# Clears of the retention heads' row tiles set between POOL's copies, and the heads' sums of squares and absolute totals made on POOL

## The chip, the cores and the metric

The kernel runs on one core of a Trainium2 chip. The metric is the time of one execution in microseconds (us), less is better. The core's engines work side by side and are tied by semaphores: PE (matmul; its weight loads are listed as PEld), DVE (vector), ACT (activation), POOL (GpSimd) and SP, which here issues DMAs. All tensors are float32.

## The reference, cut to what matters

The program is a chain of small layers over 2048 tokens of 128 channels: a causal attention layer, a spline layer, the retention layer (`L0_attn_b`), the spline layer again, linear attention, and two blocks of causal attention with a mixture of experts round an RWKV layer. The change is inside the retention layer, which computes

```python
q, k = split(x @ W_qk + b_qk);  v = x @ W_v + b_v          # 16 heads: 8 wide for q and k, 16 wide for v
mask = decay / sqrt(decay.sum(-1))                          # causal, one decay rate for each head
scores = einsum('bhtd,bhsd->bhts', q, k) * mask
denom = clip(abs(scores).sum(-1), 1.0, 50000.0)             # one absolute total for each token and head
ret = einsum('bhts,bhsv->bthv', scores / denom, v)
ret = ret * rsqrt(mean(ret * ret, axis=-1) + EPS)           # mean over the 16 values of a head
out = ((x @ W_g + b_g) * ret) @ W_o + b_o
```

The kernel puts the decays into q and k. It takes `ret` without the denominator, by a running state, and brings `denom` in at the end.

## The kernel before

`retention_layer` works on `NT` = 16 tiles of 128 tokens and `H` = 16 heads with `VD` = 16 values each. Four steps matter here, each one or more blocks; a block ends when every engine is through with it, and the next begins for all of them after that.

**The linear stage** (`chunk_stage` with `inner=False`) goes over the 16 tiles of tokens. For a tile `i`, POOL copies 128 columns of the turned q (`tile_q_t`, L1522), DVE copies the tile's k (`tile_k`, L1613) and ACT its v (`tile_v`, L1666). PE multiplies k by v (`state_ps`, L1561), DVE multiplies that by a mask into the next `state` (L1632), and PE multiplies q by the state (`tile_out_ps`, L1579), which ACT copies to `ret_out` (L1660). On PE the product of tile `i` stands ahead of the output of tile `i - 2`. There are four slots, so POOL's copy and DVE's copy for tile `i` both wait for the output of tile `i - 4`. DVE's order is: state of tile `i`, then k of tile `i + 2`. POOL's copies run in a hardware loop from tile 4 on.

The same block also makes ready the row tiles of the next stage, `head_q` and `head_k`, each of 128 partitions by two halves (`par` 0 and 1, for even and odd heads) by 2048 tokens. SP loads the rows of heads 0 and 1 into partitions 0 to 31. `RetentionRows.pad` clears partitions 32 to 63 and 64 to 127 of both tiles on POOL, four instructions over both halves at once, after the last copy (L1542). Half 1 of `head_q` served as a store for the parts that were written to memory before, so its clear has to wait until those are stored (`wait_parts`).

**The heads** (`retention_heads_stage`). For each head PE computes k by q products into `abs_dve_ps` and `abs_act_ps`. Four of them, on the diagonal, DVE multiplies by a causal mask into `own_scores` (L1966); the rest only feed the absolute totals: ACT sums into slot 0 of `abs_part` (L1940), DVE into slots 1 and 2 (L1972, 14 for a head). POOL makes `own_positive` = max(`own_scores`, 0) (L1849) after it has copied the head's v into `ret_v_head` (L1848). During head `h`, from DVE's product 8 on, PE computes the diagonal output of head `h - 1` from `own_scores` and `own_positive`; ACT copies it, PE turns it, and after product 16 DVE adds it to `ret_out` (L1957) and copies column 16 of it, the diagonal's share of the absolute total, to `abs_diag` (L1958). Both add 1 to `o_used`. POOL multiplies the head's 16 columns of `ret_gate` by `ret_out` (`gate_head`, L1842) as soon as L1957 is done. POOL's order is: gate product of head `h - 2`, v of head `h`, `own_positive` of head `h`.

**The norm** (`HeadNorm`) opens the output stage. ACT squares all of `ret_out`. DVE sums the three slots of `abs_part` for all heads, adds `abs_diag`, clips and takes the reciprocal (L2021 to L2024), sums the squares over each head's 16 values (L2026), and makes the factor `ret_ms` for each token and head (L2027 to L2032). Then it scales `ret_gate` (L2036), and PE turns and projects it. Each of DVE's steps waits for the one before it (`Chain`).

**The output stage** (`output_stage`) turns, projects and adds to `x`.

## Time and profile before

| | us |
|---|---|
| runs | 2369.28, 2376.51, 2373.66 |
| median | 2373.66 |
| the profiled execution | 2371.53 |
| its span in the trace | 2369.8 |

| engine | busy us | share of the span |
|---|---|---|
| PE | 1926.9 | 81% |
| DVE | 1669.7 | 70% |
| ACT | 1374.1 | 58% |
| POOL | 462.9 | 20% |

A share of the whole span is a mean over stages with different limits, so it doesn't say what bounds one stage. For the change, three stretches of the timeline count, in us from the span's start: the linear stage from about 617 to 653, the heads from 653 to 874, and the norm from 874 to 886. In a timeline row the bracket says how long the engine had been idle before the row and whose work ended that; in a row of windows, the number after the engines' busy times is the clock granted to PE, where 1.00 is 2.4 GHz and 0.50 is 1.2 GHz.

### The profile page before, as it was taken

How to read it: one execution, taken by the hardware profiler on the slowest of the kernel's cores; microseconds unless marked ns; L12 is line 12 of the kernel's file. 1: busy time of each engine (PE TensorE's matmuls, PEld its weight loads, DVE VectorE, ACT ScalarE, POOL GpSimd, SP SyncE). 2: the span in 40 equal slices, each digit the busy share in tenths (PEclk: the TensorE clock that was granted, in tenths of full speed). 3: DMA queues.
4: the chain of work that ended last, by engine and by line, in shares of the span. 5: the costliest groups of instructions: out<-in, count | busy, mean ns of one | idle time of the engine just before them, and what ended most of it. 6: DMA issues, size and time to landing. Idle time of an engine off the chain costs nothing. (4 is left out here: it accounts for less than half of the span.)

```text
span 2369.8 us, 38818 instructions
## 1 busy us (share of the span) xinstructions
PE 1926.9 (81%) x12970; PEld 1039.0 (44%) x12970; DVE 1669.7 (70%) x4197; ACT 1374.1 (58%) x2027; POOL 462.9 (20%) x816
## 2 busy tenths in 40 slices
PE   4899899975699974687899899957647999999839
PEld 3433333333477753464333333337334333333338
DVE  6798898747366777467798898632697887888423
ACT  4257767865388865435366677832544466677712
POOL 4110120110355430220101110133001010211233
PEclk9599999996899986897699999978866799999959
DMA  7242030001201000006132030014114411300034
GB/s 228 74 72 36 5 38 2 2 23 42 89 29 40 38 18 1 1 1 178 23 51 38 3 38 2 2 47 170 33 44 134 72 16 25 37 3 2 2 105 162
DMA packets 47527, 113.89 MB, mean 48 GB/s; under 512 B 11952, under 2 KB 21426, under 8 KB 43144
## 3 DMA queue, kind: packets, MB, share of 16 engines
q1 hardware_dynamic: 40308, 96.84, 17.4%
q0 software_dynamic: 5088, 11.24, 1.5%
q10 hardware_dynamic: 1964, 3.70, 0.4%
q8 instruction: 90, 1.47, 0.3%
q14 instruction: 77, 0.63, 0.1%
HBM read 62.39 MB, written 32.64 MB: 40 GB/s over the span
## 5 line engine op out<-in xcount | busy, mean ns | idle before, releaser
L1125 ACT ACTIVATE probs<-score 128x1024 f32<-128x1024 f32 x960 | 822.8, 897 | 428.1 <-PE score L1224 422.3
L1295 DVE TENSOR_REDUCE max_part<-stat 128x1 f32<-128x512 f32 x1152 | 724.4, 682 | 95.3 <-PE stat L1176 87.5
L1238 PE MATMUL pv<-probs,v_ones 128*9 128x512 f32 (+3 forms) x3840 | 457.7, 550 | 0.6 <-ACT out_turned L1118 0.6
L1292 DVE CUSTOM_DVE_ANT_0 masked_scores<-stat,mask_row 128x128 f32<-128x128 f32 (+3 forms) x768 | 346.9, 487 | 145.7 <-PE stat L1176 142.4
L1176 PE MATMUL stat<-first_group_k,first_group_q 64*128 64x512 f32 (+2 forms) x960 | 364.0, 493 | 36.3 <-DVE max_part L1295 13.0
L1176 PE MATMUL stat<-group_k,group_q 64*128 64x512 f32 (+2 forms) x960 | 337.6, 407 | 16.1 <-DVE max_part L1295 7.6
L1176 PEld LDWEIGHTS stat<-first_group_k,first_group_q 64*128 64x128 f32 x960 | 175.9, 214 | 283.4 <-DVE max_part L1295 174.3
L1176 PEld LDWEIGHTS stat<-group_k,group_q 64*128 64x128 f32 x960 | 157.9, 185 | 279.1 <-DVE max_part L1295 161.1
L1224 PE MATMUL score<-first_group_q,first_group_k 64*128 64x512 f32 x960 | 250.2, 421 | 32.0 <-ACT probs L1125 19.6
L1224 PE MATMUL score<-group_q,group_k 64*128 64x512 f32 x960 | 230.1, 418 | 40.5 <-ACT probs L1125 31.2
L1083 POOL TENSOR_SCALAR_AFFINE_SELECT probs<-probs 128x256 f32<-128x256 f32 x384 | 150.1, 408 | 235.7 <-ACT probs L1125 234.3
L1940 ACT ACTIVATE abs_act_ps<-abs_act_ps 128x1024 f32<-128x1024 f32 (+3 forms) x176 | 167.5, 952 | 43.4 <-PE abs_act_ps L1895 39.8
L1224 PEld LDWEIGHTS score<-first_group_q,first_group_k 64*128 64x128 f32 x960 | 131.2, 198 | 53.7 <-ACT probs L1125 29.6
L1224 PEld LDWEIGHTS score<-group_q,group_k 64*128 64x128 f32 x960 | 112.9, 186 | 89.5 <-ACT probs L1125 84.5
L1972 DVE TENSOR_REDUCE abs_part<-abs_dve_ps 128x512 f32 (+5 forms) x224 | 108.9, 515 | 60.7 <-PE abs_dve_ps L1909 60.6
L1895 PE MATMUL abs_act_ps<-head_k,head_q 128*128 128x512 f32 x352 | 117.8, 420 | 1.4 <-ACT abs_act_ps L1940 0.2
L1092 POOL CAST row_max_parts<-row_max 128x16 fp32r<-128x16 f32 x48 | 9.5, 198 | 559.6 <-DVE row_max L1269 559.6
L1238 PEld LDWEIGHTS pv<-probs,v_ones 128*9 128x9 f32 x3840 | 57.4, 88 | 120.3 <-issue 89.6
L2444 DVE TENSOR_TENSOR hidden<-value_ps,gate 128x512 f32<-128x512 f32 x38 | 26.3, 691 | 116.8 <-PE value_ps L2348 116.8
L1100 POOL TENSOR_TENSOR qkv<-out_rows,inv_denominator 128x128 f32<-128x128 f32 x48 | 19.6, 408 | 373.1 <-DVE inv_denominator L1276 373.1
L1849 POOL TENSOR_SCALAR own_positive<-own_scores 128x2048 f32<-128x2048 f32 x16 | 85.8, 5362 | 0.0
L1909 PE MATMUL abs_dve_ps<-head_k,head_q 128*128 128x512 f32 (+2 forms) x224 | 71.9, 346 | 0.0
(375 smaller groups left out, 2476.0 us busy)
## 6 DMA issues: line engine op xcount, KB each, us to landing
tile_wv<-expert_wv SPq DMA_DIRECT2D x38, 512.0 KB, 3.3
q_parts<-early_parts_t SPq DMA_DIRECT2D x14, 512.0 KB, 3.8
group_k<-k_parts SPq DMA_DIRECT2D x24, 256.0 KB, 11.9
group_q<-q_parts SPq DMA_DIRECT2D x24, 256.0 KB, 18.4
k_parts<-early_parts_t SPq DMA_DIRECT2D x8, 512.0 KB, 4.5
head_q<-q_parts SPq DMA_DIRECT2D x32, 128.0 KB
head_k<-k_parts SPq DMA_DIRECT2D x32, 128.0 KB
first_group_q<-pad_rows SPq DMA_DIRECT2D x6, 512.0 KB, 5.5
```

The lines of the kernel that those rows point to most:

```text
L1083: nc.gpsimd.affine_select(tile, tile, [[0, 2], [1, P]], ALU.is_ge, 0.0, base=0, channel_multiplier=-1).then_inc(cut.sem, 1)
L1125: nc.scalar.activation(probs[:, n % PSLOTS, :, 0:width], sc[m % 2][:, :, 0:width], ACT.Exp, scale=scale).then_inc(slot_read.sem, 1)
L1176: nc.tensor.matmul(ring[n % RBANKS][:, 0:width], rounded(uq[b][rows, h // 2, at:at + P]), rounded(uk[b][rows, h // 2, c * BANK:c * BANK + ...
L1224: last = nc.tensor.matmul(sc[m % 2][:, i, 0:BANK - f], rounded(uk[b][rows, hp, kt * P:(kt + 1) * P]), rounded(uq[b][rows, hp, j * BANK + f ...
L1238: last = nc.tensor.matmul(acc[32 * h:32 * h + D + 1, f:BANK], v9[:, kt, g * HG + h, :], probs[:, (2 * t + h // 2) % PSLOTS, h % 2, 0:BANK ...
L1292: nc.vector.tensor_tensor_reduce(masked[:, at % 2, 0:width], ring[n % RBANKS][:, 0:width], w["mask_row"][:, BANK - width:BANK], 1.0, NEG, ...
L1295: nc.vector.reduce_max(into, ring[n % RBANKS][:], AX.X).then_inc(stat_used.sem, 1)
L1849: nc.gpsimd.tensor_scalar(sa[:, par, :], sm[:, par, :], 0.0, None, ALU.max).then_inc(abs_ready.sem, 1)
L1895: ins = nc.tensor.matmul(a_ps[slot][:, b:min(b + BANK, width)], rounded(qm[:, par, i * P:(i + 1) * P]), rounded(km[:, par, at + b:at + min ...
L1909: ins = nc.tensor.matmul(out[:, 0:width], rounded(qm[:, par, i * P:(i + 1) * P]), rounded(km[:, par, at:at + width]), start=True, stop=True)
L1940: nc.scalar.activation(ps, ps, ACT.Abs, accum_out=part[:, bass.ds(h, 1), i, 0:1]).then_inc(a_used.sem, 1)
L1972: nc.vector.tensor_reduce(part[:, bass.ds(h, 1), i, slot:slot + 1], d_ps[n % DRING][:, 0:width], AX.X, ALU.add, apply_absolute_value=True) ...
```

## The change

It has three parts.

1. `pad` becomes a generator of eight clears, each over one half of a tile (2048 elements in a partition in place of 4096), in the order `head_k`, `head_q` for half 0, then for half 1. In the linear stage POOL's loop is unrolled, and one clear follows each of the copies for tiles 4 to 11. After each copy POOL waits until the copy is done, and after each clear until the clear is done. The wait for the stored parts stands only ahead of the two clears of `head_q`'s half 1. The copies for tiles 12 to 15 have no clear behind them.
2. `gate_head` waits for both of DVE's increments (L1958 too), and after the gate product POOL sums this head's part: the squares of its 16 columns of `ret_out`, halved three times and then added into `ret_ms`, and the three slots of `abs_part` with `abs_diag`, clipped into `ret_den`. That is nine POOL instructions for each of heads 0 to 14, in two chains that alternate, where each waits for the instruction two places before it. POOL's loop over heads is unrolled.
3. `HeadNorm` makes the square, the absolute total, the clip and the sum of squares for head 15 alone. The two reciprocals and the products over all heads stay.

```diff
@@ chunk_stage, POOL
-                with pool.Fori(1, NT // SLOTS) as n:
-                    for slot in range(SLOTS):
-                        body(SLOTS * n + slot, slot)
-                if ahead:
-                    wait_parts(pool, parts_stored(k))
-                    pool.wait_ge(staged.sem, staged.at(NS * NT))
-                    ahead.pad(pool)
+                if inner:
+                    with pool.Fori(1, NT // SLOTS) as n:
+                        for slot in range(SLOTS):
+                            body(SLOTS * n + slot, slot)
+                else:
+                    pads = ahead.pad(pool, parts_stored(k))
+                    for i in range(SLOTS, NT):
+                        body(i, i % SLOTS)
+                        pool.wait_ge(staged.sem, staged.at(i + 1))
+                        next(pads, None)
@@ class RetentionRows
-    def pad(self, pool):
-
-        n = 0
-        for tile in (self.q, self.k):
-            for unused in (slice(KROWS, 2 * KROWS), slice(2 * KROWS, P)):
-                n += 1
-                self.nc.gpsimd.memset(tile[unused].rearrange("r b t -> r (b t)"), 0.0).then_inc(self.padded.sem, 1)
-                pool.wait_ge(self.padded.sem, self.padded.at(n))
+    def pad(self, pool, stored):
+
+        pieces = [(tile, par, unused) for par in range(2) for tile in (self.k, self.q) for unused in (slice(KROWS, 2 * KROWS), slice(2 * KROWS, P))]
+        for n, (tile, par, unused) in enumerate(pieces):
+            if tile is self.q and par == 1:
+                wait_parts(pool, stored)
+            self.nc.gpsimd.memset(tile[unused, par, :], 0.0).then_inc(self.padded.sem, 1)
+            pool.wait_ge(self.padded.sem, self.padded.at(n + 1))
+            yield
@@ retention_heads_stage, POOL
-                def gate_head(h):
-
-                    pool.wait_ge(o_used.sem, o_used.at(2 * h + 1))
-                    g, r = (t[:, :, bass.ds(h * VD, VD)] for t in (gate, ret))
+                def gate_head(h, first=False, sums=True):
+
+                    pool.wait_ge(o_used.sem, o_used.at(2 * h + 2))
+                    g, r = (t[:, :, h * VD:(h + 1) * VD] for t in (gate, ret))
                     nc.gpsimd.tensor_tensor(g, g, r, ALU.mult).then_inc(gated.sem, 1)
+                    if sums:
+                        sum_head(h, r, first)
+
+                def sum_head(h, r, first):
+
+                    one = part[:, h:h + 1, :, :].rearrange("p o t s -> p (o t) s")
+                    own = diag[:, h:h + 1, :].rearrange("p o t -> p (o t)")
+                    square_sum, abs_sum = (t[:, :, h:h + 1].rearrange("p t o -> p (t o)") for t in (ms, den))
+
+                    def done(n):
+                        pool.wait_ge(summed.sem, summed.at(h * NSUM + n))
+
+                    if not first:
+                        done(0)
+                    nc.gpsimd.tensor_tensor(sq[:], r, r, ALU.mult).then_inc(summed.sem, 1)
+                    nc.gpsimd.tensor_tensor(total[:], one[:, :, 0], one[:, :, 1], ALU.add).then_inc(summed.sem, 1)
+                    done(1)
+                    nc.gpsimd.tensor_tensor(sq[:, :, 0:8], sq[:, :, 0:8], sq[:, :, 8:16], ALU.add).then_inc(summed.sem, 1)
+                    done(2)
+                    nc.gpsimd.tensor_tensor(total[:], total[:], one[:, :, 2], ALU.add).then_inc(summed.sem, 1)
+                    done(3)
...
+                    done(7)
+                    nc.gpsimd.tensor_tensor(square_sum, sq[:, :, 0], sq[:, :, 1], ALU.add).then_inc(summed.sem, 1)
...
-                with pool.Fori(1, H // 2) as n:
-                    for par in range(2):
-                        gate_head(2 * n + par - 2)
-                        body(2 * n + par, par)
+                for h in range(2, H):
+                    gate_head(h - 2, first=h == 2)
+                    body(h, h % 2)
                 gate_head(H - 2)
-                gate_head(H - 1)
+                gate_head(H - 1, sums=False)
@@ class HeadNorm
-        nc.scalar.activation(self.sq[:], self.ret[:], ACT.Square).then_inc(self.squared.sem, 1)
+        nc.scalar.activation(self.sq[:], self.ret[:, :, (H - 1) * VD:], ACT.Square).then_inc(self.squared.sem, 1)
...
-        by_head = den[:].rearrange("p t h -> p h t")
-        chain(nc.vector.tensor_reduce(by_head, self.part[:], AX.X, ALU.add))
-        chain(nc.vector.tensor_tensor(by_head, by_head, self.diag[:], ALU.add))
-        chain(nc.vector.tensor_scalar(den[:], den[:], 1.0, 50000.0, ALU.max, ALU.min))
+        last = den[:, :, H - 1]
+        chain(nc.vector.tensor_reduce(last, self.part[:, H - 1], AX.X, ALU.add))
+        chain(nc.vector.tensor_tensor(last, last, self.diag[:, H - 1], ALU.add))
+        chain(nc.vector.tensor_scalar(last, last, 1.0, 50000.0, ALU.max, ALU.min))
         chain(nc.vector.reciprocal(den[:], den[:]))
         dve.wait_ge(self.squared.sem, self.squared.at(1))
-        chain(nc.vector.tensor_reduce(ms[:], sq[:].rearrange("p t (h v) -> p t h v", v=VD), AX.X, ALU.add))
+        chain(nc.vector.tensor_reduce(ms[:, :, H - 1], sq[:], AX.X, ALU.add))
```

What stands in a row on POOL at the end of the linear stage, before: the loop's last copy of q, the loop's end, the four clears, the block's end.

```order
L1522 COPY tile_q_t<-ret_q_t 128x128
L1536 REGISTER_ALU
L1536 COMPARE_AND_BRANCH
L1759 MEMSET head_q 32x4096
L1759 MEMSET head_q 64x4096
L1759 MEMSET head_k 32x4096
L1759 MEMSET head_k 64x4096
L1508 UNCONDITIONAL_BRANCH
```

The same engine from the first copies of the stage on, now (tiles 0 to 7; half 1 is cleared in the same manner, and four copies and the block's end follow):

```order
L1522 COPY tile_q_t<-ret_q_t 128x128 x5
L1762 MEMSET head_k 32x2048
L1522 COPY tile_q_t<-ret_q_t 128x128
L1762 MEMSET head_k 64x2048
L1522 COPY tile_q_t<-ret_q_t 128x128
L1762 MEMSET head_q 32x2048
L1522 COPY tile_q_t<-ret_q_t 128x128
L1762 MEMSET head_q 64x2048
```

The clears moved from behind the last copy to between the copies, in eight halves. On POOL in the heads, one head before, from the gate product of head `h - 2` to `own_positive` of head `h` (ISA and REGISTER_ALU belong to the loop):

```order
L1842 TENSOR_TENSOR ret_gate<-ret_gate,ret_out 128x16x16
L1846 REGISTER_ALU
L1847 ISA
L1848 ISA
L1848 COPY ret_v_head<-ret_qkv 128x16x16
L1849 TENSOR_SCALAR own_positive<-own_scores 128x2048
```

And now:

```order
L1848 TENSOR_TENSOR ret_gate<-ret_gate,ret_out 128x16x16
L1863 TENSOR_TENSOR own_squared<-ret_out 128x256
L1864 TENSOR_TENSOR own_abs_total<-abs_part 128x16
L1866 TENSOR_TENSOR own_squared<-own_squared 128x16x8
L1868 TENSOR_TENSOR own_abs_total<-own_abs_total,abs_part 128x16
L1870 TENSOR_TENSOR own_squared<-own_squared 128x16x4
L1872 TENSOR_TENSOR own_abs_total<-own_abs_total,abs_diag 128x16
L1874 TENSOR_TENSOR own_squared<-own_squared 128x16x2
L1876 TENSOR_SCALAR ret_den<-own_abs_total 128x16
L1878 TENSOR_TENSOR ret_ms<-own_squared 128x16
L1884 COPY ret_v_head<-ret_qkv 128x16x16
L1885 TENSOR_SCALAR own_positive<-own_scores 128x2048
```

Nine instructions came in between the gate product and the copy of v. On DVE the norm, before:

```order
L2021 TENSOR_REDUCE ret_den<-abs_part 128x16x16
L2022 TENSOR_TENSOR ret_den<-ret_den,abs_diag 128x16x16
L2023 TENSOR_SCALAR ret_den<-ret_den 128x256
L2024 RECIPROCAL ret_den<-ret_den 128x256
L2026 TENSOR_REDUCE ret_ms<-ret_sq 128x256
L2027 SCALAR_TENSOR_TENSOR ret_ms<-ret_ms,ret_den 128x256
```

And now:

```order
L2056 TENSOR_REDUCE ret_den<-abs_part 128x16
L2057 TENSOR_TENSOR ret_den<-ret_den,abs_diag 128x16
L2058 TENSOR_SCALAR ret_den<-ret_den 128x16
L2059 RECIPROCAL ret_den<-ret_den 128x256
L2061 TENSOR_REDUCE ret_ms<-ret_sq 128x16
L2062 SCALAR_TENSOR_TENSOR ret_ms<-ret_ms,ret_den 128x256
```

No instruction moved here; four of the six became a sixteenth as large.

## Rows read from the trace of the kernel before

**Rows 1.** Timeline, end of the linear stage: start, length, engine, names, count, [idle before].

```profile
623.00 0.29 POOL L1522 COPY tile_q_t<-ret_q_t 128x128 f32 x1 [4.64 <-PE tile_out_ps L1579]
624.81 0.30 POOL L1522 COPY tile_q_t<-ret_q_t 128x128 f32 x1 [1.52 <-PE tile_out_ps L1579]
...
637.88 0.29 POOL L1522 COPY tile_q_t<-ret_q_t 128x128 f32 x1 [0.98 <-PE tile_out_ps L1579]
638.33 7.07 POOL L1759 MEMSET head_q<- 32x4096 f32 x2
645.46 7.07 POOL L1759 MEMSET head_k<- 32x4096 f32 x2
...
641.47 0.37 ACT L1660 COPY ret_out<-tile_out_ps 128x256 f32<-128x256 f32 x1 [0.36 <-PE tile_out_ps L1579]
...
653.03 1.09 PE L1905 MATMUL abs_dve_ps<-head_q,head_k 128*128 128x128 f32 x4 [11.60 <-PEq L1508]
```

**Rows 2.** Windows and timeline, the heads: busy us of each engine, clock; steady head.

```profile
662.00:869.00 207.00, 205.37 (x1820) 149.33 (x1818) 147.25 (x308) 179.20 (x358) 103.39 (x46) 1.00 0.09 36
...
748.81 2.49 DVE L1966 TENSOR_TENSOR own_scores<-abs_dve_ps,keep_kq 128x512 f32<-128x512 f32 x4
...
748.54 0.75 POOL L1842 TENSOR_TENSOR ret_gate<-ret_gate,ret_out  x1 [4.70 <-DVE abs_diag L1958]
751.47 0.40 POOL L1848 COPY ret_v_head<-ret_qkv 128x256 f32 x1 [2.18 <-DVE own_scores L1966]
```

**Rows 3.** Timeline, from the last gate product through the norm before the output stage.

```profile
873.14 0.72 POOL L1842 TENSOR_TENSOR ret_gate<-ret_gate,ret_out 128x256 f32<-128x256 f32 x1 [3.30 <-DVE abs_diag L1958]
...
874.22 0.95 DVE L2021 TENSOR_REDUCE ret_den<-abs_part 128x256 f32<-128x768 f32 x1 [1.07 <-PEq L1813]
...
876.16 1.75 DVE L2024 RECIPROCAL ret_den<-ret_den 128x256 f32<-128x256 f32 x1
...
882.40 0.42 DVE L2027 SCALAR_TENSOR_TENSOR ret_ms<-ret_ms,ret_den 128x256 f32<-128x256 f32 x1
```

**Rows 4.** Groups by shape, POOL: count | busy us, mean ns | idle before.

```profile
L1532 POOL MEMSET tile_v<- 128x2048 f32 x1 | 1.8, 1806 | 32.1 <-POOLq L566 32.1
...
L1093 POOL TENSOR_TENSOR row_max_parts<-row_max,row_max_parts 128x16 fp32r<-128x16 f32 x48 | 10.7, 222 | 4.0 <-POOL row_max_parts L1092 0.2
```

**Rows 5.** One line each: DVE copy, DVE sum (ns min/median/max); POOL product in time.

```profile
L1613 DVE COPY tile_k<-ret_qkv x16: 164/227/310, 617.6 to 637.7; 128x128 f32<-128x128 f32 x8, 128x128 f32 x8
...
L1431 DVE SCALAR_TENSOR_TENSOR spline_sum<-spline_knot,W,spline_sum x56: 731/740/2786, 539.6 to 938.8; 128x512 f32<-128x512 f32 x56
...
537.34 4.51 POOL L1417 TENSOR_TENSOR X<-X,bout 128x2048 f32<-128x2048 f32 x1 [20.79 <-ACT xn L371]
```

**Rows 6.** Windows round the linear stage: busy us of each engine, granted clock.

```profile
616.00:619.00 3.00, 0.89 (x4) 0.30 (x2) 0.93 (x5) 2.32 (x7) 1.07 (x4) 1.00 0.18 68
619.00:623.00 4.00, 3.18 (x7) 1.93 (x8) 1.33 (x6) 0.14 (x1) 0.00 (x1) 0.56 0.13 41
...
626.00:641.00 15.00, 13.10 (x48) 8.11 (x48) 6.65 (x21) 7.78 (x23) 6.24 (x11) 0.99 0.12 48
...
653.00:660.00 7.00, 6.97 (x27) 6.52 (x28) 3.48 (x6) 2.70 (x6) 3.23 (x7) 0.50 0.00 1
...
957.00:965.00 8.00, 5.02 (x29) 4.30 (x29) 3.40 (x7) 2.82 (x7) 0.00 (x0) 0.98 0.00 0
```

**Rows 7.** Timeline, DVE in the first head: first and fourth product.

```profile
654.23 0.69 DVE L1966 TENSOR_TENSOR own_scores<-abs_dve_ps,keep_kq 128x512 f32<-128x512 f32 x1 [15.21 <-PE abs_dve_ps L1905]
...
658.00 0.69 DVE L1966 TENSOR_TENSOR own_scores<-abs_dve_ps,keep_kq 128x512 f32<-128x512 f32 x1 [0.80 <-PE abs_dve_ps L1905]
```

**Rows 8.** One line: DVE products beside POOL work, ns min/median/max.

```profile
L1966 DVE TENSOR_TENSOR own_scores<-abs_dve_ps,keep_kq x64: 677/680/693, 654.2 to 857.9; 128x512 f32<-128x512 f32 x64
```

**Rows 9.** Groups by shape, DVE: small operations like the new ones.

```profile
L1972 DVE TENSOR_REDUCE abs_part<-abs_dve_ps 128x256 f32 x42 | 17.7, 421 | 12.0 <-PE abs_dve_ps L1909 12.0
...
L2409 DVE TENSOR_TENSOR pick<-pick,picked_so_far 128x16 f32<-128x16 f32 x4 | 0.7, 170 | 0.1
```

More of the change, by code:

```diff
@@ L1764, in done, with retention_heads_stage @@
             sig.done(self.COUNT * H // 2)
-        self.padded.done(4)
-def retention_heads_stage(k, w, v, rows, part, diag, ret, gate, x):
+        self.padded.done(8)
+def retention_heads_stage(k, w, v, rows, part, diag, ret, gate, den, ms, x):
     nc = k.nc
@@ L1997, in retention_heads_stage, with __init__ @@
         gated.done(H)
+        summed.done(NSUM * (H - 1))
 class HeadNorm:
-    def __init__(self, k, w, part, diag, ret, gate, ctx):
+    def __init__(self, k, w, part, diag, ret, gate, den, ms, ctx):
         self.k, self.part, self.diag, self.ret, self.gate = k, part, diag, ret, gate
-        self.den = k.sb("ret_den", [P, NT, H], F32, ctx)
-        self.sq = k.sb("ret_sq", [P, NT, H * VD], F32, ctx)
-        self.ms = k.sb("ret_ms", [P, NT, H], F32, ctx)
+        self.den, self.ms = den, ms
+        self.sq = k.sb("ret_sq", [P, NT, VD], F32, ctx)
         self.step, self.scaled = k.counter("scale_step"), k.counter("rows_scaled")
@@ L2523, in retention_layer @@
                 chunk_stage(k, w, qkv[:, :, C:2 * C], qkv[:, :, 2 * C:], q_t, None, VD, w["bd16"][:], ret, inner=False, ahead=rows)
-        retention_heads_stage(k, w, qkv[:, :, 2 * C:], rows, part, diag, ret, gate, x)
+        retention_heads_stage(k, w, qkv[:, :, 2 * C:], rows, part, diag, ret, gate, den, ms, x)
         output_stage(k, w, [(gate[:, :, b * C:(b + 1) * C], w["w_o_r"][:, b, :]) for b in range(2)], x,
-                     norm=HeadNorm(k, w, part, diag, ret, gate, ctx))
+                     norm=HeadNorm(k, w, part, diag, ret, gate, den, ms, ctx))
 def linear_layer(k, w, x):
```

16 lines of the change are left out of this document (13 added, 3 removed).

## The prediction

> **What bounds the kernel now.** I read the timelines of three places, the windows round them for PE's clock, and the groups by shape for prices.
>
> At the end of the linear stage, see what POOL does after the last copy of q [rows 1]. The copy of tile 15 is at 637.88, then four clears run from 638.33 to 645.46 + 7.07 = 652.53. The tiles' last work, ACT's copy, ends at 641.47 + 0.37 = 641.84. PE starts the heads at 653.03 after 11.60 us idle. So the clears alone hold the block's end for 10.7 us.
>
> In the heads, see who is never idle: PE is busy for 205.37 of 207 us at full clock, POOL for 103.39 [rows 2]. PE is the bound, and POOL matters only if it comes late for PE. In a steady head POOL waits 4.70 us before the gate product at 748.54 and 2.18 us before the copy of v at 751.47 [rows 2]; 6.9 us in a head are free.
>
> In the norm everything is one chain on DVE: the first sum starts at 874.22, and L2027, the first step that isn't cut, at 882.40 [rows 3]. That is 8.18 us with nothing beside it on the path.
>
> **Part 1, the clears.** A clear of 2048 elements took 1.81 us [rows 4]. Two of the long ones took 7.07 together, 3.5 each with about 0.06 between. Eight short ones cost 14.5, as much as now, so what counts is where they lie. A tile's copy is 0.3 to 0.37, a clear 1.81, and two waits for completion some 0.06 each: POOL needs 2.3 us for a tile with a clear. The stage goes at 0.29 + 1.52 = 1.8 a tile with PE at half clock (the copy at 624.81) and at 0.3 + 0.98 = 1.28 at full clock (637.88) [rows 1]. POOL therefore sets the pace of tiles 4 to 11, and the clears are not hidden: they stretch the stage. The first of the copies stays at 623.00, the copy of tile 12 comes at 623.00 + 8 x 2.3 = 641.4. Before, it came 3 x 1.28 ahead of 637.88, at 634.04, and the stage's work ended 7.8 later. Now PE has caught up and needs no slot freed before it takes tile 12, which wins back one pace less the copy, 0.8: the end is at 641.4 + 7.8 - 0.8 = 648.4. That is 4.1 less than 652.53. Of the 10.7 us, 6.6 are given back by the slower tiles.
>
> Who waits behind a clear? On POOL the next copy, counted above. On DVE the copy of k may too. It took 164 ns at least, 227 in the median and 310 at most, and POOL's copy stands at the same moment; a DVE sum with two inputs in SBUF that began at 539.6, beside a POOL product that ran from 537.34 to 541.85, took 2786 ns where the median is 740 [rows 5]. So I take it that DVE's copy waits for the end of a running clear. The Trainium skill, in "SBUF — State Buffer" (section "SBUF: two separate sides"), says that GpSimd and VectorE share a port pair as an exclusive lock, held for the whole instruction; the sum's 2786 ns agree, and for a clear, which reads nothing, no run here shows it. The k copied there is for two tiles ahead, and it gets its turn when POOL's next copy does, so it costs 0.1 to 0.2 for a tile at most where POOL paces, which is within my rounding of 2.3.
>
> The clock is the open term. Before, it fell while PE was busy 0.89 of 3 us, and stayed up at 13.10 of 15 and at 5.02 of 8 [rows 6]. Under the clears PE has the same work for a tile, about 13.10 x 1.28 / 15 = 1.1 us at full clock, in 2.3: 0.49. That lies between the rows, nearer to 0.63 (stayed) than to 0.30 (fell), but it comes as one burst in each 2.3 us, and I hold a fall likelier than not. While it is low, the clears' pace still hides it (1.8 against 2.3). The last tiles pay: 3 paces x 0.53 = 1.6, and some 1.3 more for the last outputs if the clock doesn't come back. As these tiles run back to back at low clock, as they did when it rose at about 626, I expect it back by about the heads' start: 2.0 in all.
>
> The heads begin at half clock now: 0.50 from 653 to 660 [rows 6], after the long idle. The first head's four products took from 654.23 to 658.69, 4.46 [rows 7], where a steady head needs 2.49 [rows 2]; with the slow first matmuls ahead of them, half of the 1.20 us from 653.03 to 654.23, that is 2.5 lost by then. With an idle gap of about 1 us in place of 11.6 the clock can stay up: a gain of 2.3, or nothing if it is low then.
>
> **Part 2, the sums on POOL.** Nine instructions for a head. An operation on 16 elements took 0.22 [rows 4], the gate product on 256 took 0.75 [rows 2]. Between them by size: 0.75, 0.22, 0.45, 0.22, 0.33, 0.22, 0.27, 0.20, 0.22 = 2.9, to 3.3 with the waits. Taken all as dear as the gate product they would be 6.8, still under the 6.9 free. In the steady head they end at 748.54 + 0.1 + 0.75 + 3.1 = 752.5, 1.0 after the copy of v is made now. So `own_positive` ends at 758.6 in place of 757.2, and PE wants it a head later, well after. Cost: nothing, with more than 6 us of cover. The wait for L1958 adds 0.1 to a gate product that nobody waits for, but for the last. At the end POOL was idle 3.30 before the last gate product [rows 3]: sums of 2.9 to 3.3 for head 14 just fit there. With the 0.1 this costs 0.1 to 0.3; I take 0.2.
>
> The Trainium skill's "GPSIMD Engine Reference" (section "3.1 Elementwise — side-by-side cycle accounting") gives VectorE as the engine for elementwise work, since GpSimd takes about twice as long for a two-input sum. Going by that, the sums should stay where they were; on this path it is the idle engine that counts, not the faster one.
>
> **Part 3, the norm.** In place of 8.18: a sum of 3 for each of 16 (about 0.2), two operations on 16 elements (0.17 each [rows 9]), the reciprocal 1.75 [rows 3], a sum over 256 elements 0.42 [rows 9], five gaps of 0.04: 2.9. ACT's square of 256 elements is done long before. Gain 5.3, less the 0.2 above: 5.1. What is late next is the reciprocal itself, which stays.
>
> **The sum** against the profiled execution, 2371.53 (span 2369.8, 1.7 us outside it): clears 4.1, low clock in the last tiles -2.0, heads at full clock 2.3, norm 5.1: 9.5, giving 2362.0. The median of the runs is 2.13 above the profiled one, so against it I forecast 2373.66 - 9.5 = 2364.2.
>
> **Rivals.** (a) The clock never falls under the clears (the share 0.49 is nearer to the row that stayed): 4.1 + 2.3 + 5.1 = 11.5, 2362.2. (b) It falls and is still low when the heads begin, as it was for 7 us before: 4.1 - 2.9 + 0 + 5.1 = 6.3, 2367.4. (c) DVE's copy of k waits for a clear each time and the state behind it too, and PE for that, in series: each of the eight tiles takes 2.3 + 1.28 and the stage ends 8 x 1.28 = 10.2 later than 648.4, 6.1 later than before. With the norm's 5.1 that is 1.0 slower, 2374.7. Against it: the copy is two tiles ahead of its use. (d) Slower: the sums on POOL hold up DVE's products L1966, which run at 748.81 to 751.30 just beside them. If these had to wait for the POOL chain, up to 2.5 us a head x 14 = 35 less 9.5, 2399; it decides from 9.5 / 14 = 0.7 us a head on. Against it: the gate product, which reads and writes the same kind of tiles, overlaps the first of them (748.54 to 749.29), and all 64 took 677 to 693 ns [rows 8].
>
> **How the numbers follow.** Forecast 0.36, (a) 0.24, (b) 0.22, (c) 0.08, (d) 0.03, the rest 0.07 for small things not seen, either way. The runs before differ by 7.2 us, so 1 to 2 us of chance go on top of each case. The range 2359 to 2371 holds the forecast, (a) and (b) with that. A measurement can tell about 0.3%, 7.1 us: 2366.5. Faster by more than that: nearly all of (a), most of the forecast, a quarter of (b), 0.62. Slower: (d), part of (c) and the rest, 0.05. Within: 0.33.
>
> **What would show it.** Right: POOL's timeline with eight clears of 1.8 between copies 2.3 apart; the linear stage's end 4 to 1 us earlier and then PE idle for about 1 us; no wait of PE for `own_positive`, a head's period unchanged; L2027's counterpart 2.9 us after the norm's first sum. The granted clock from 630 to 660 tells (a), the forecast and (b) apart. Wrong: k copies or products of DVE of over 1 us with the state late by a whole clear, heads longer than before, or POOL's sums over 6.9 us a head.

## The result: 18.8 us less than before, 10 below the forecast

The changed kernel took 2354.13 us, the median of 5 runs (2351.16 to 2363.12), the kernel before 2372.91 beside it (5 runs). The ratio is 0.9934, with a 95% interval from 0.9910 to 0.9957. The direction was forecast, the size was not: 2364.2 was expected, and 2354.13 lies below the range of 2359 to 2371. Timed again beside the kernel before, it gave 0.9958 [0.9936, 0.9979] (median 2362.55) and 0.9925 [0.9898, 0.9952] (2358.07). The mean of the three ratios is 0.9939, 14.5 us. The first interval, 10.2 to 21.4 us, and the third, 11.4 to 24.2, hold what the touched stretches gave (13.3 us, below) and not the 9.5 us forecast; the second, 5.0 to 15.2, holds both.

The profiled execution took 2354.56 us, with a span of 2352.8 and 2369.8 before. I cut both spans at four points that both kernels have: POOL's first copy of q in the linear stage, POOL's clear of `abs_part` that opens the heads' block, the norm's first sum on DVE, and the step that multiplies `ret_ms` by `ret_den`.

| stretch | before | after | gain |
|---|---|---|---|
| first copy of q to the heads' first clear | 35.70 | 30.59 | 5.11 |
| heads' first clear to the norm's first sum | 221.23 | 218.32 | 2.91 |
| first sum to the first step of the norm that isn't cut | 8.18 | 2.92 | 5.26 |
| from there to the end | 1487.4 | 1483.3 | 4.1 |
| start to the first copy of q | 617.3 | 617.7 | -0.4 |

The three stretches that the change touches gave 13.3 us. The last two hold nothing of it; I return to them below.

POOL's timeline at the end of the linear stage, after (start, length, engine, names, count, idle time before). It answers to [rows 1].

```profile
634.39 0.29 POOL L1522 COPY tile_q_t<-ret_q_t 128x128 f32<-128x128 f32 x1
634.74 1.80 POOL L1762 MEMSET head_k<- 64x2048 f32 x1
636.60 0.29 POOL L1522 COPY tile_q_t<-ret_q_t 128x128 f32<-128x128 f32 x1
...
639.17 1.80 POOL L1762 MEMSET head_q<- 64x2048 f32 x1
641.03 0.70 POOL L1522 COPY tile_q_t<-ret_q_t 128x128 f32<-128x128 f32 x2
642.70 0.29 POOL L1522 COPY tile_q_t<-ret_q_t 128x128 f32<-128x128 f32 x1 [0.96 <-PE tile_out_ps L1582]
643.97 0.29 POOL L1522 COPY tile_q_t<-ret_q_t 128x128 f32<-128x128 f32 x1 [0.98 <-PE tile_out_ps L1582]
648.24 0.74 POOL L1833 MEMSET abs_part<- 128x768 f32 x1 [3.97 <-POOLq L1508]
```

Copies and clears follow one another without idle time, one tile every 2.21 us (634.39 to 636.60). That is POOL setting the pace, as forecast. The double row at 641.03 is tiles 12 and 13: PE has caught up, and their slots are free at once. From there POOL waits for PE again, and the heads' block opens 4.27 us after the last copy.

Now the windows over the same time, with the busy time of PE, PEld, DVE, ACT and POOL and then PE's granted clock. They answer to [rows 6].

```profile
634.00:636.00 2.00, 1.13 (x4) 0.68 (x4) 0.83 (x2) 0.47 (x3) 1.88 (x3) 1.00 0.12 49
636.00:637.00 1.00, 0.05 (x1) 0.05 (x1) 0.59 (x1) 0.67 (x2) 0.88 (x3) 0.94 0.12 49
637.00:638.00 1.00, 1.00 (x3) 0.82 (x4) 0.00 (x0) 0.00 (x0) 1.00 (x1) 0.50 0.16 66
638.00:639.00 1.00, 1.00 (x3) 0.30 (x1) 0.42 (x1) 0.00 (x0) 0.94 (x2) 0.50 0.12 49
639.00:640.00 1.00, 0.86 (x3) 0.75 (x3) 0.81 (x1) 0.68 (x2) 0.94 (x2) 0.50 0.08 33
640.00:641.00 1.00, 0.83 (x3) 0.34 (x2) 1.00 (x2) 0.04 (x1) 0.97 (x1) 0.86 0.00 0
...
648.00:655.00 7.00, 6.48 (x37) 5.28 (x38) 5.09 (x11) 5.20 (x11) 5.26 (x7) 1.00 0.01 2
```

The clock stood at its upper level, 2.4 GHz, while PE was busy 1.13 of 2 us, and it did fall, near 636.9, to 0.50 (1.2 GHz). But it was up again near 640.3, before the copy of tile 12. The low stretch lay wholly under the clears, which hid it. The heads began at 1.00, where before they began at 0.50 [rows 6].

POOL in a steady head, after, beside the gate product and the copy of v of [rows 2]:

```profile
848.14 0.74 POOL L1848 TENSOR_TENSOR ret_gate<-ret_gate,ret_out 128x256 f32<-128x256 f32 x1 [4.63 <-DVE abs_diag L1993]
848.84 0.61 POOL L1863 TENSOR_TENSOR own_squared<-ret_out 128x256 f32<-128x256 f32 x1
...
851.07 0.21 POOL L1878 TENSOR_TENSOR ret_ms<-own_squared 128x16 f32<-128x16 f32 x1
851.23 0.39 POOL L1884 COPY ret_v_head<-ret_qkv 128x256 f32<-128x256 f32 x1
```

The nine sums take from 848.84 to 851.23, 2.39 us. Nearly all of that was POOL's wait before the copy of v, 2.18 us before and none now. DVE's products beside them kept their length of [rows 8], in one row for all 64, with the shortest, the median and the longest in ns:

```profile
L2001 DVE TENSOR_TENSOR own_scores<-abs_dve_ps,keep_kq x64: 677/680/692, 649.0 to 850.2; 128x512 f32<-128x512 f32 x64
```

Last, the timeline of POOL and DVE from the last gate product to the norm, after, which answers to [rows 3]:

```profile
865.49 0.72 POOL L1848 TENSOR_TENSOR ret_gate<-ret_gate,ret_out 128x256 f32<-128x256 f32 x1 [0.82 <-DVE abs_diag L1993]
...
866.56 0.20 DVE L2056 TENSOR_REDUCE ret_den<-abs_part 128x16 f32<-128x48 f32 x1 [1.15 <-PEq L1819]
866.80 0.18 DVE L2057 TENSOR_TENSOR ret_den<-ret_den,abs_diag 128x16 f32<-128x16 f32 x1
867.02 0.18 DVE L2058 TENSOR_SCALAR ret_den<-ret_den 128x16 f32<-128x16 f32 x1
867.24 1.75 DVE L2059 RECIPROCAL ret_den<-ret_den 128x256 f32<-128x256 f32 x1
869.02 0.42 DVE L2061 TENSOR_REDUCE ret_ms<-ret_sq 128x16 f32<-128x256 f32 x1
869.48 0.43 DVE L2062 SCALAR_TENSOR_TENSOR ret_ms<-ret_ms,ret_den 128x256 f32<-128x256 f32 x1
```

From 866.56 to 869.48 are 2.92 us. POOL still waited 0.82 us before the last gate product, so head 14's sums held nothing up.

### The profile page after: what moved, and what is told of

It reads as the page before. It is cut to its first block and busy times, and to the rows that moved or that the text cites. A ratio compares the mean times of both kernels' runs of the same rounds, so it can differ in the third digit from the quotient of the medians.

```text
span 2352.8 us, 38871 instructions
## 1 busy us (share of the span) xinstructions
PE 1920.1 (82%) x12963; PEld 1033.4 (44%) x12970; DVE 1666.7 (71%) x4197; ACT 1370.3 (58%) x2027; POOL 497.4 (21%) x955
## 6 DMA issues: line engine op xcount, KB each, us to landing
group_k<-k_parts SPq DMA_DIRECT2D x24, 256.0 KB, 12.2
```

## The experiments

Each row is one profiled execution, with its span cut at the same points. The lengths of stages below are from this table. "Rest" is what follows the norm's first uncut step, which is the same code in every kernel.

| kernel | linear stage | heads | norm's sums | rest |
|---|---|---|---|---|
| before | 35.70 | 221.23 | 8.18 | 1487.4 |
| after | 30.59 | 218.32 | 2.92 | 1483.3 |
| after, again | 31.30 | 217.99 | 2.91 | 1488.8 |
| after, third | 30.61 | 218.11 | 2.92 | 1489.5 |
| clears alone | 31.31 | 218.24 | 8.18 | 1497.0 |
| sums alone | 35.71 | 221.39 | 2.92 | 1478.5 |
| clears moved, first | 24.81 | 218.30 | 2.92 | 1482.2 |
| clears moved, again | 24.81 | 218.19 | 2.92 | 1485.5 |
| two clears early | 29.80 | 218.35 | 2.92 | 1487.4 |
| two clears a copy | 35.36 | 218.28 | 2.91 | 1491.4 |
| clears late | 31.32 | 218.31 | 2.92 | 1488.7 |
| sums twice | 31.30 | 219.80 | 2.91 | 1490.4 |
| sums three times | 31.32 | 229.58 | 2.92 | 1487.5 |

Five kernels ran only once each: two clears early 2359.39 us, two clears a copy 2369.67, clears late 2360.73 and sums three times 2371.30, beside 2371.86 for the kernel before, and sums twice 2371.95, beside 2375.78. A single time says little here, so these five are read from their stretches alone.

**The changed kernel once more, and its two parts apart.** The first kernel is the changed one, without an edit.

> The changed kernel once more, for a narrower ratio. Theory A (what the two traces show up to the norm, 13 us, is all there is; the further 4 us between the profiled executions lie in attention layers that the change doesn't touch, and come and go from one execution to the next): 12 to 14 us below before, ratio about 0.9945. Theory B (the later layers gain too): 16 to 17 us, ratio about 0.993.

The second has the change in POOL's part of the linear stage and in `RetentionRows`, and the heads and the norm of before:

```diff
-                with pool.Fori(1, NT // SLOTS) as n:
-                    for slot in range(SLOTS):
-                        body(SLOTS * n + slot, slot)
...
+                    pads = ahead.pad(pool, parts_stored(k))
+                    for i in range(SLOTS, NT):
+                        body(i, i % SLOTS)
+                        pool.wait_ge(staged.sem, staged.at(i + 1))
+                        next(pads, None)
```

> Part 1 alone: the clears between the copies, the sums where they were before. Theory A: the heads' block begins about 5 us sooner and, with PE at full clock from its start, the norm begins about 7.7 us sooner: 7 to 8 us below before. The prediction's forecast for this part was 4.1 - 2.0 + 2.3 = 4.4. Theory B: more than 9 us.

The third has the change in the heads and the norm, and the clears of before:

```diff
-                def gate_head(h):
+                def gate_head(h, first=False, sums=True):
...
+                    if sums:
+                        sum_head(h, r, first)
...
-        chain(nc.vector.tensor_reduce(by_head, self.part[:], AX.X, ALU.add))
+        chain(nc.vector.tensor_reduce(last, self.part[:, H - 1], AX.X, ALU.add))
```

> Parts 2 and 3 alone: the sums on POOL and the short norm, the clears behind the last copy as before. Theory A: 5.1 us below before, the linear stage and the first head unchanged, a head's period unchanged. Rival: the sums make the heads longer and what the norm gains is partly eaten: 0 to 3 us.

Against 2374.79 us for the kernel before (29 runs), the changed kernel took 2362.55 (12 runs, 0.9958 [0.9936, 0.9979]), the clears alone 2364.60 (12 runs, 0.9951 [0.9931, 0.9971]) and the sums alone 2368.33 (12 runs, 0.9976 [0.9956, 0.9996]). The changed kernel's 12.2 us are those of its theory A. The clears alone are 10.2 us below before by the medians, which taken alone would be theory B, with an interval from 6.9 to 16.4 that holds A too; their stretches give 7.4, which is A. The sums alone are 6.5 us below (0.9 to 10.4), where 5.1 was expected. By the table the clears give 4.4 us in the linear stage and 3.0 in the heads and nothing in the norm. The sums give 5.3 in the norm, and nothing of the rest: 35.71 and 221.39 are within 0.2 us of before. The parts add up, 7.4 + 5.1 = 12.5, to what both give in the profile of the changed kernel taken beside them, 12.9. So the 2.9 us in the heads belong to the clears, which end before the heads begin; it is the clock, and not the sums: with the sums alone PE's clock was at 0.50 from the heads' start at 655.47 to 662, and with the clears alone at 1.00 from their start on.

The medians can't tell the two parts apart: the clears' interval and that of both together overlap almost wholly. The profiles show why. The rest ran 9.6 us longer than before's with the clears alone and 8.9 shorter with the sums alone, and it is the same code.

**The clock comes back at different times.** The repeated profile of the changed kernel has 31.30 in place of 30.59. Its timeline of POOL:

```profile
646.04 0.65 POOL L1522 COPY tile_q_t<-ret_q_t 128x128 f32<-128x128 f32 x2
648.60 0.29 POOL L1522 COPY tile_q_t<-ret_q_t 128x128 f32<-128x128 f32 x1 [1.91 <-PE tile_out_ps L1582]
649.61 0.29 POOL L1522 COPY tile_q_t<-ret_q_t 128x128 f32<-128x128 f32 x1 [0.72 <-PE tile_out_ps L1582]
653.88 0.74 POOL L1833 MEMSET abs_part<- 128x768 f32 x1 [3.97 <-POOLq L1508]
```

And its windows:

```profile
640.00:642.00 2.00, 0.92 (x5) 0.46 (x4) 1.02 (x2) 0.68 (x2) 1.88 (x3) 0.93 0.14 57
642.00:644.00 2.00, 2.00 (x4) 1.13 (x4) 0.42 (x1) 0.00 (x0) 1.94 (x2) 0.50 0.12 49
644.00:646.00 2.00, 1.86 (x5) 1.17 (x4) 1.79 (x2) 0.68 (x2) 1.92 (x2) 0.50 0.04 16
646.00:648.00 2.00, 1.86 (x5) 1.17 (x4) 0.77 (x4) 0.68 (x2) 0.59 (x2) 0.50 0.00 0
648.00:650.00 2.00, 1.82 (x8) 1.19 (x7) 0.95 (x4) 1.07 (x4) 0.59 (x2) 0.86 0.00 0
```

Here the clock stayed low past the copy of tile 12 at 646.04 and until about 648.6. From that copy to the heads' first clear it took 653.88 - 646.04 = 7.84 us, and in the first profile 648.24 - 641.03 = 7.21. So a late return costs 0.6 us more than an early one, which costs nothing that can be seen. Of the six profiles with this order of clears two were early (30.59, 30.61) and four late (31.30 to 31.32). The Trainium skill, in "TensorE: Matmul & The Clock Gate" (section "Part 1: The HAM clock gate"), says that the moment of a change of clock varies from run to run of one kernel; these profiles agree, with 3.4 us at low clock in the first and 6.8 in the repeated one.

**The clears taken out of the linear stage.** Six clears go to POOL in the stage that projects q, k and v, after its first projection, where POOL has nothing to do. The two that have to wait until the parts are stored go to the heads' start, ahead of POOL's work for head 0, and PE waits for them before head 1.

```diff
+            if clear:
+                @block.gpsimd
+                def _(pool):
+                    pool.wait_ge(projected.sem, projected.at(1))
+                    clear.pad(pool, False)
...
-                    pads = ahead.pad(pool, parts_stored(k))
                     for i in range(SLOTS, NT):
                         body(i, i % SLOTS)
-                        pool.wait_ge(staged.sem, staged.at(i + 1))
-                        next(pads, None)
...
                 pool.wait_ge(cleared.sem, cleared.at(5))
+                rows.pad(pool, True)
```

> The changed kernel with the clears taken out of the linear stage: six of the eight stand on POOL in the block before it, where POOL is idle, from the first projection on, and the last two (half 1 of head_q) at the start of the heads, ahead of head 0's own work; PE waits for them before head 1. If the POOL-paced tiles are what is left of the clears' cost, the linear stage takes 8 x (2.21 - 1.28) = 7.4 us less less what tiles regained, so about 6 us: 18 to 20 us below before. Rival: POOL's clears hold up DVE's products of two tiles in SBUF in the block where they now stand, and half of that is lost.

It took 2353.77 (6 runs, 0.9915 [0.9888, 0.9942]). Timed again:

> The kernel with six clears on POOL in the stage before the linear stage and two at the heads' start, again. Its linear stage was 24.81 us from first copy to the heads' first clear (30.6 to 31.3 in the changed kernel) and its heads 218.30. Theory: 5.8 to 6.5 us less than the changed kernel in the same call, a ratio to the kernel before of about 0.992. Rival (the six earlier clears only move the cost ahead of the linear stage): the same time as the changed kernel.

and beside it the changed kernel a third time:

> The changed kernel unaltered, timed beside the two others of this call and the kernel before. Its stages gave 13.3 and 12.9 us in two profiles (5.1 and 4.4 in the linear stage, 2.9 and 3.2 in the heads, 5.3 in the norm) while the medians gave 18.8 us in one comparison and 12.2 in another. Theory (the change is worth its stages, the rest is chance in layers that it does not touch): a ratio that holds 0.9945 (13 us), and later layers in the profile that lie some us on either side of the kernel before. Rival (the change also speeds up later layers, by about 4 us as in the first pair of profiles): 17 us, 0.993, and in the profile 4 us less from the norm to the end again.

The kernel before took 2375.78 there (12 runs), the changed one 2358.07 (7 runs, 0.9925 [0.9898, 0.9952]) and this one 2348.95 (6 runs, 0.9895 [0.9863, 0.9928]). It was 8.8 and 9.1 us faster than the changed kernel beside it; the table gives 5.8 to 6.5 of that, and the rest is as uncertain as before. Its stage, 24.81 us in both profiles, is the linear stage with no clear in it. So in the changed kernel the eight clears still cost 5.8 us, or 6.5 with the clock late. The 5.8 can be followed: the eight paced tiles take 17.77 us (623.26 to 641.03) and here 11.05 (625.25 to 636.30), where the first two still go at 1.80 because PE is at low clock; that is 6.7, of which the catching up wins back 0.96. POOL's timeline at its heads' start:

```profile
644.47 0.74 POOL L1834 MEMSET abs_part<- 128x768 f32 x1 [3.98 <-POOLq L1514]
...
646.84 3.66 POOL L1764 MEMSET head_q<- 32x2048 f32 x2
650.56 0.40 POOL L1886 COPY ret_v_head<-ret_qkv 128x256 f32<-128x256 f32 x1
```

The copy of v for head 0 comes 6.09 us after the block's start in place of 3.58 (651.82 in the changed kernel), and the heads are none the longer, 218.30. The expectation's rival, that the six clears cost the earlier stage as much, would have brought the time of the changed kernel; it did not. The traces say the same: from POOL's last work in the layer before (its sum into `X`) to the first copy of q, with that earlier stage in between, it took 79.93 us with the six clears there (539.73 to 619.66) and 79.94 in the changed kernel (537.71 to 617.65).

The third profile of the changed kernel bears on the other question. Its ratio, 0.9925, lies nearer to the rival's 0.993 than to the 0.9945 of the theory, and its interval holds both. Its rest was 2.1 us longer than that of before, where in the first pair it was 4.1 shorter, and 1.4 longer in the repeated one. So the profiles show no sign that the change speeds up later layers; the ratio by itself does not exclude it.

**Two clears where POOL waits.** POOL waits 4 us between its first four copies and the fifth.

```diff
                     pads = ahead.pad(pool, parts_stored(k))
+                    pool.wait_ge(staged.sem, staged.at(SLOTS))
+                    for _ in range(2):
+                        next(pads, None)
```

> The changed kernel with two of the eight clears taken out from between POOL's copies and put right behind the first four copies, where POOL waited 4 us for the fifth; six stay behind copies 4 to 9. Theory (what a clear costs is the pace of its tile, 2.21 - 1.28 = 0.93 us, wherever POOL paces, and nothing where POOL waits): from POOL's first copy to its first clear of the heads, 30.6 to 31.3 us in the changed kernel, falls by 2 x 0.93 = 1.9, to 28.7 to 29.4. Rival (the stage pays for POOL's total work, so it does not matter where a clear lies): 30.6 to 31.3. Rival (the early clears hold up DVE's first copies of k and so the start of the stage): over 31. The granted clock falls under the clears as in the changed kernel and is back before the last tiles; the heads begin at 1.00.

29.80 us. That is 1.5 below the profiles with a late clock and 0.8 below the early ones, and 0.4 above what was expected. Most of what is missing is the clock, low from 638 to 642 (0.57 and 0.58 in the two windows), when the clears were over: from copy 10 to the heads' first clear it took 10.76 us (638.16 to 648.92), and 10.81 in the kernel without clears (633.66 to 644.47), although PE had caught up. The rest is 0.14 at the start: two of DVE's copies of k beside the early clears took 1.32 and 1.53 us, and POOL's copy of tile 4 came 5.75 us after its first copy in place of 5.61. That is the second rival, held up as it says, at a small price. Where a clear lies does decide: here two clears where POOL waits cost 0.14 us together, and 0.93 each between the copies.

**Two clears behind each of four copies.**

```diff
-                        next(pads, None)
+                        for _ in range(2):
+                            next(pads, None)
```

> The changed kernel with two clears behind each of copies 4 to 7 in place of one behind each of copies 4 to 11. Theory of the pace: each of four tiles takes 0.37 + 2 x 1.84 = 4.05 us, 4 x (4.05 - 1.28) = 11.1 us over a stage without clears where eight tiles of 2.21 cost 7.4: from first copy to the heads' first clear 3.7 longer than in the changed kernel, 34.3 to 35.0 us, if the clock costs nothing. The clock is the second question: PE has 1.1 us of work in 4.05, a share of 0.27, near the row where it fell (0.30), so it should fall early; if it then stays low for some of tiles 8 to 15, these cost 0.53 each, up to 4 more, 35 to 39. Rival (only the number of clears counts, 8 x 1.8): 30.6 to 31.3.

35.36 us, with the same eight clears, 4.1 to 4.8 more than the changed kernel. The copies came 4.06 to 4.13 us apart. Four tiles of 4.07 cost more than eight of 2.21, since each paced tile hides only its own 1.28 us. The windows show the clock:

```profile
632.00:634.00 2.00, 0.00 (x0) 0.00 (x0) 0.00 (x0) 0.00 (x0) 1.94 (x2) 0.59 0.16 57
634.00:636.00 2.00, 1.94 (x4) 1.18 (x4) 0.42 (x1) 0.00 (x0) 1.88 (x3) 0.50 0.14 57
...
644.00:646.00 2.00, 2.00 (x6) 1.28 (x5) 0.76 (x2) 0.68 (x2) 0.29 (x1) 0.50 0.00 0
646.00:648.00 2.00, 1.82 (x9) 1.29 (x8) 1.15 (x4) 1.35 (x4) 0.59 (x2) 0.99 0.00 0
```

It was low from 632 to 646. The last clear ended at 641.78, so about 4 us of unhidden work ran at half clock. From copy 8 (641.85) to the heads' first clear (655.30) it took 13.45 us, the same as the 13.37 of the kernel with no clears (631.10 to 644.47), though PE had caught up, which is worth 0.96 in the first profile of after (8.17 without clears, 7.21 there, from copy 12 on). So the clock cost 1.0 us.

**The clears last.**

```diff
-                        next(pads, None)
+                        if i >= 8:
+                            next(pads, None)
```

> The changed kernel with the eight clears behind copies 8 to 15 in place of 4 to 11, so that the tiles that POOL paces are the last. It tests the two clock terms of the prediction (-2.0 for the last tiles and their outputs, and 2.3 for heads that begin at full clock). By the pace alone: 8 x 0.93 = 7.4, and the 0.8 that the catching up wins back in the changed kernel is not there, so 31.4 to 32.1 us from first copy to the heads' first clear, and the heads' block as long as in the changed kernel, 218.3. Theory of the clock as predicted: it falls under the clears, and with no tile behind them at full pace it stays low: the last outputs take 1.3 us more (32.7 to 33.4) and the heads begin at 0.50, which costs the heads' block 2.3 to 3, as before (about 221). Rival: it comes back by itself: neither.

31.32 us and 218.31. The windows and PE's timeline at the end of the stage:

```profile
644.00:646.00 2.00, 1.80 (x5) 0.99 (x4) 0.42 (x1) 0.37 (x1) 1.88 (x3) 0.50 0.00 0
646.00:648.00 2.00, 2.00 (x7) 1.35 (x6) 0.00 (x0) 0.56 (x2) 1.02 (x1) 0.68 0.00 0
648.00:650.00 2.00, 1.28 (x9) 0.87 (x8) 0.09 (x1) 0.56 (x2) 0.82 (x2) 1.00 0.00 0
```

```profile
645.22 1.22 PE L1565 MATMUL state_ps<-tile_v,tile_k 128*128 128x256 f32 x2 [0.20 <-POOL tile_q_t L1522]
646.23 2.22 PE L1583 MATMUL tile_out_ps<-state,tile_q_t 128*128 128x256 f32 x6
```

The same outputs in the changed kernel:

```profile
645.80 1.75 PE L1582 MATMUL tile_out_ps<-state,tile_q_t 128*128 128x256 f32 x6
```

This is the nearest to what I had forecast, and both halves of it can be read. The clock was low for the last tile and for most of the last outputs. PE's last work took from 645.22 to 648.45, 3.23 us, where the changed kernel needs 2.26 (645.29 to 647.55): 1.0 lost, near the 1.3 forecast. But the expectation denied that PE catches up here, and it does. PE starts the last tile 0.35 us after POOL's copy (644.87 to 645.22), and 1.32 in the changed kernel (643.97 to 645.29): 1.0 won. The two cancel, and only seven of the eight clears lie between copies: 24.81 + 7 x 0.93 = 31.32, the measured length. And the heads began at full clock: it rose in the last outputs, in a window in which PE was busy 2.00 of 2 us. Even with the clears at the very end no time in the heads was lost.

**The sums twice and three times.** The nine sums of a head are made over again, with the same result. For three times:

```diff
-    OW, NSUM = 32, 9
+    OW, TURNS = 32, 3
+    NSUM = 9 * TURNS
...
+                    for turn in range(TURNS):
+                        once(h, r, first and turn == 0, one, own, square_sum, abs_sum, 9 * turn)
```

> The changed kernel with the nine sums of each head made three times over (same result), so 7.4 us of sums in a head in place of 2.45. It tests that POOL has 6.9 us free in a head, and that the cost appears at the end. Theory: POOL's work in a head is then 0.5 us over what is free. If that makes POOL the bound each head is 0.5 us longer, 7 us in 14 heads; and the sums of head 14 hold the last gate product, where POOL has 0.82 us idle now: 2 x 2.45 - 0.82 = 4.1 us later. Heads' block from its first clear to the norm's first sum: 218.3 + 4.1 = 222.4 if POOL has more cover than the 6.9 that the idle time shows, 229.5 if it has not. Rival (DVE's products are held by POOL's sums, rival d): over 230, and L2001's products over 1 us.

229.58 us, the 229.5 of a POOL that becomes the bound. Its rows:

```profile
841.98 0.73 POOL L1849 TENSOR_TENSOR ret_gate<-ret_gate,ret_out 128x256 f32<-128x256 f32 x1
...
850.47 5.36 POOL L1893 TENSOR_SCALAR own_positive<-own_scores 128x2048 f32<-128x2048 f32 x1
855.91 0.73 POOL L1849 TENSOR_TENSOR ret_gate<-ret_gate,ret_out 128x256 f32<-128x256 f32 x1
```

The gate product has no idle time before it any more, and a head takes 855.91 - 841.98 = 13.93 us, where the changed kernel needs 861.53 - 848.14 = 13.39.

For twice the edit is the same with `TURNS` 2.

> The changed kernel with the nine sums of each head made twice, 4.9 us of sums in a head, below the 6.9 that POOL has free. With three times 2.45 the heads became 0.67 us longer each. Theory (6.9 us are free, and the cost appears only where the sum passes it): a head as long as in the changed kernel, and only the last gate product comes later, by 2.45 less the 0.82 us for which POOL waits before it: heads' first clear to the norm's first sum 218.3 + 1.6 = 219.9. Rival (POOL's sums cost in proportion from the start): half of what three times cost, 5.6 us, 223.9.

219.80 us, where 219.9 was expected from the end alone, and in each head POOL waits again before the gate product:

```profile
843.30 0.74 POOL L1849 TENSOR_TENSOR ret_gate<-ret_gate,ret_out 128x256 f32<-128x256 f32 x1 [2.03 <-DVE abs_diag L2001]
```

So 6.9 us are free in a head, as [rows 2] showed: 4.9 us cost nothing there and 7.4 cost half a us a head. (The 0.67 us for a head in that expectation was too high; the gate products above give 0.54.)

## Why the prediction was right and wrong

**The pace of the tiles** was right in kind: POOL sets it for tiles 4 to 11. Its size was 2.3 in the prediction and is 2.21, since the waits cost less than allowed. Over eight tiles that is 0.7 us.

**The catching up** was right. From copy 12 to the end of the stage's work 7.8 - 0.8 = 7.0 us were forecast; 641.03 to 647.59 + 0.37 are 6.93.

**The clock in the last tiles** is the term of the sum that failed most: -2.0. Its parts were 1.6 and 1.3, 2.9 together, and no working leads from 2.9 to the 2.0; it was a guess at how much would be over in time. The fall itself was forecast, and it came. What I mis-sized was how long it lasts and what meets it. I let it reach over the last tiles and part of the outputs, and it lasted 3.4 us in the first profile, all of it under the clears, and 6.8 in the second, of which the first 4.3 lay under them. It cost 0 and 0.6 us in place of 2.0. The step went wrong where it charged low clock to the last tiles because the clears end there; the clock had fallen long before they ended and had come back under them or soon behind. Rival (a) gave 0 for this term by another mechanism, that the clock never falls. Its number was nearer, its reason was false.

**The heads' start** at full clock was forecast as 2.3 and gave 2.9. The copy of v for head 0 comes 3.58 us after the block's start, where it was 5.84: 2.26, which is the 2.3. The copy before, and after:

```profile
658.83 0.40 POOL L1848 COPY ret_v_head<-ret_qkv 128x256 f32<-128x256 f32 x1 [3.54 <-DVE own_scores L1966]
```

```profile
651.82 0.40 POOL L1884 COPY ret_v_head<-ret_qkv 128x256 f32<-128x256 f32 x1 [1.27 <-DVE own_scores L2001]
```

The other 0.6 came after the point at which I stopped counting: before, the clock stayed at 0.50 until 660 [rows 6], 1.2 us beyond that copy at 652.99 + 5.84 = 658.83, and half of that was lost too. Rival (b), low clock at the heads' start, is excluded even with the clears last.

**The sums on POOL** were right: no cost in a head, DVE's products unchanged, so rival (d) is excluded. Estimated at 2.9 to 3.3 us they take 2.4, and the 0.2 for head 14's sums at the end was nothing: 0.82 us remain free there. The end of `own_positive` at 758.6 was a slip, since 1.0 after 757.2 is 758.2; nothing hangs on it. It now comes only 0.15 us later against the gate product: 8.66 us behind its start before (748.54 to 757.20), 8.81 after (848.14 to 856.95).

**The norm** was right: 5.3 forecast, 5.26 measured.

**Rival (c)**, DVE's copies of k held by the clears, was right in its first half and wrong in its price. The copies are held, as the last section shows. The state behind them is not, but for once, where it took 0.63 us in place of 0.42 (once 1.05 with the clears last), and the copies are two tiles ahead of their use.

In the forecast's terms the sum was 4.1 - 2.0 + 2.3 + 5.1 = 9.5. By the first profile it is 5.1 + 2.9 + 5.3 = 13.3, and by the three profiles of the changed kernel 13.3, 12.9 and 13.5. Their mean of 13.2, taken off 2373.66, would have given 2360.5, which lies inside the range. So the mis-sized terms are 3.7 of the 10.1 us by which the forecast missed the first median. The other 6.3 us, which carried it out of the range, are not explained by the change, and the experiments show of what kind they are. The three medians of the changed kernel were 2354.13, 2362.55 and 2358.07. The rest behind the norm, the same code throughout, took from 1478.5 to 1497.0 us in thirteen profiles. So a second step failed: I added "1 to 2 us of chance" to each case, and a median of five moves by several. Even with the right sum, the range should have reached 6 to 7 us to either side of it. The record has one hint of what moves: PE's mean granted clock of a run goes with its time. Of the 12 runs of the changed kernel the fastest, 2351.51 us, had 0.891 and the slowest, 2372.83, had 0.876; of the 29 of the kernel before these were 2365.80 with 0.887 and 2382.01 with 0.878. In which layers the clock is lost, and whether that is the cause, was not looked into and stays open. It is not the layers behind the norm alone: the first copy of q came between 617.3 and 625.8 us in the thirteen profiles, though the last 79.9 us before it were the same in all.

## What to carry to other kernels

Work put between the steps of an engine that then sets the pace is not hidden: each step grows by the work's length less what the step can hide, and it costs least where the engine already waits. Look first for such a place, in the stage before if need be: here the eight clears cost 5.8 us between the copies, and nothing that the traces show with six of them one stage earlier and two at the heads' start. If an engine idles long at a stage's end, ask what the next stage's clock is after it; removing the idle time can give more than the idle time alone, here 2.9 us more.

Compare stretches between fixed points of two profiles, and not only spans or medians, where a change is worth some tenths of a per cent: each stretch here repeated within 0.4 us or showed two clear levels, while medians of the same kernel differed by 8.4 us.

## What the hardware showed

DVE's copy of k, from SBUF to SBUF, waits for a running clear on POOL, though a clear reads nothing. DVE's timeline of the changed kernel:

```profile
636.03 0.59 DVE L1616 COPY tile_k<-ret_qkv 128x128 f32 x1
638.21 0.42 DVE L1635 TENSOR_TENSOR state<-state_ps,bd 128x256 f32<-128x256 f32 x1 [1.59 <-PE state_ps L1564]
639.20 1.85 DVE L1616 COPY tile_k<-ret_qkv 128x128 f32 x1 [0.56 <-PE tile_out_ps L1582]
640.42 0.63 DVE L1635 TENSOR_TENSOR state<-state_ps,bd 128x256 f32<-128x256 f32 x1
```

The copy at 639.20, 0.03 us after the clear that began at 639.17, ended at 641.05, just behind the clear's end at 640.97. The median copy took 227 ns before, with 310 at most [rows 5]. The one at 636.03 ended at 636.62, behind a clear that ended at 636.54. The product that updates the state, with one input in PSUM, took 0.42 beside a clear; the one at 640.42 came behind the held copy and ended with it. The prediction cited the Trainium skill, "SBUF — State Buffer" (section "SBUF: two separate sides"), for the exclusive lock of the port pair and said that no run showed it for a clear. These rows now agree with it for a clear too: DVE's copy is held until an operation that only writes has ended. The copy that began first, at 627.93, 0.16 us ahead of a clear, took its usual 0.23.

The clock rose again at 640.3 while POOL still paced PE, with PE busy 2.86 of 3 us at half clock in the three windows from 637 to 640. Before the fall PE had been busy 1.13 of 2 us with the same work for a tile (634 to 636). So at low clock the same work fills nearly all of PE's time, and the clock came back without the load having changed. That is why the fall cost so little here. Whether the fuller PE brings the clock back is not shown: in the repeated profile PE was busy 5.72 of 6 us from 642 to 648, just as full, and the clock rose only near 648.6. Why one takes 3.4 us and the other 6.8 stays open.
